# When the reciprocals of the softmax row sums are taken: sixteen quarter-reciprocals per batch, spread over the slots of the attention loop

## The reference, cut to what matters

```python
q, k, v = ...                       # (b, heads 8, t 2048, 32); expert e = tokens e*512..(e+1)*512
attn = jnp.einsum('bhqd,bhkd->bhqk', q, k) * scale
attn = jax.nn.softmax(attn, axis=-1)                      # exp(s - max) / sum
attn_out = jnp.einsum('bhqk,bhkd->bhqd', attn, v)
...
for e in range(4):                  # expert e uses only its first m = 256 >> e columns
    xm = attn_out[:, sl, :m]        # so expert 0 needs 8 heads, 1: 4, 2: 2, 3: 1
    out = jnp.einsum('bnm,om->bno', xm, o_w[:m, :m]) + o_b[:m]
```

## Time and profile before

| | |
|---|---|
| median of three runs | 2130.2 us |
| profiled execution, its own time | 2130.56 us |
| its span, first to last instruction | 2128.7 us |
| mean granted TensorE clock | 0.938 |
| TensorE matmul busy | 1811.4 us, 85% |
| VectorE busy | 1507.0 us, 71% |
| ScalarE busy | 1084.6 us, 51% |
| GpSimd busy | 993.4 us, 47% |

### The profile page before, as it was taken

The page is one execution under the profiler, slowest core; times in us unless marked ns, Lnnn a source line. Parts: engine busy times, 40 slices in busy tenths (PEclk is TensorE's granted clock), DMA queues, the critical chain, the costliest instruction groups (busy, mean ns, idle before and its releaser), DMA issues.

```text
span 2128.7 us, 37884 instructions
## 1 busy us (share of the span) xinstructions
PE 1811.4 (85%) x10752; PEld 1043.2 (49%) x10752; DVE 1507.0 (71%) x2733; ACT 1084.6 (51%) x1998; POOL 993.4 (47%) x654
## 2 busy tenths in 40 slices
PE   4788869999688886999968878699996887789998
PEld 3566434444366543444437654344434664434443
DVE  5688677777478676777648867777755876777774
ACT  0576333666367522566637643256653673326664
POOL 0332345666423245566733313656672332356666
PEclk8899988999899987999979999799997999889999
DMA  3000043010200015201020002500111000350011
GB/s 118 1 0 1 1 158 88 16 43 4 81 1 0 1 38 167 47 11 46 11 71 1 0 1 81 161 12 16 38 51 32 0 0 1 111 134 9 16 39 40
DMA packets 55741, 87.73 MB, mean 41 GB/s; under 512 B 13188, under 2 KB 32004, under 8 KB 52868
## 3 DMA queue, kind: packets, MB, share of 16 engines
q1 hardware_dynamic: 55560, 85.54, 13.8%
HBM read 49.68 MB, written 35.70 MB: 40 GB/s over the span
## 4 chain that ended last, share of the span: by engine, by line
PE 61%; DVE 19%; ACT 8%; issue 7%; DMA 1%; SPq 1%; POOL 1%; DVEq 1%; ACTq 0%; POOLq 0%
PE PS L1119 11%; PE PS L1244 10%; PE PS L1232 9%; PE PS L1257 5%; PE PS L1017 5%; PE PS L1049 4%; DVE MXP L829 4%; DVE XSQ L780 3%; PE PS L1041 3%; ACT XSQ L576 3%; PE PS L1021 3%; PE PS L1162 2%; PE PS L1189 2%; ACT QKT L536 1%; DVE X L732 1%
## 5 line engine op out<-in xcount | busy, mean ns | idle before, releaser
L829 DVE TENSOR_REDUCE MXP<-PS 128x1 f32<-128x512 f32 x960 | 598.9, 681 | 201.9 <-PE PS L1119 198.4
L486 POOL TENSOR_TENSOR TS<-PR 128x1024 f32<-128x1024 f32 (+1 forms) x256 | 573.2, 2239 | 329.3 <-ACT PR L647 329.3
L647 ACT ACTIVATE PR<-PS 128x512 f32<-128x512 f32 x960 | 506.0, 602 | 417.9 <-PE PS L1232 416.4
L1119 PE MATMUL PS<-KOP,QOP 96*128 96x512 f32 x960 | 423.0, 461 | 43.8 <-DMA KOP<-k_scr 30.8
L1232 PE MATMUL PS<-QOP,KOP 97*128 97x512 f32 x960 | 379.8, 409 | 14.5 <-ACT PR L647 9.7
L1119 PEld LDWEIGHTS PS<-KOP,QOP 96*128 96x128 f32 x960 | 191.1, 200 | 298.6 <-DVE MXP L829 224.4
L1244 PE MATMUL PS<-PR,V 128*32 128x512 f32 x1920 | 273.1, 605 | 0.0
L1049 PE MATMUL PS<-PB,QKT 128*128 128x512 f32 x768 | 223.3, 427 | 26.6 <-DVE QKT L760 26.6
L1232 PEld LDWEIGHTS PS<-QOP,KOP 97*128 97x128 f32 x960 | 181.3, 192 | 82.0 <-ACT PR L647 50.6
L443 POOL TENSOR_SCALAR PK<-XSK 128x1024 f32<-128x1024 f32 x64 | 67.1, 1049 | 281.2 <-ACT XSK L562 281.2
L1049 PEld LDWEIGHTS PS<-PB,QKT 128*128 128x128 f32 x768 | 142.2, 192 | 70.0 <-DVE QKT L760 39.4
(11 more groups left out here) (143 smaller groups left out, 2586.6 us busy)
## 6 DMA issues: line engine op xcount, KB each, us to landing
KOP<-k_scr SPq DMA_DIRECT2D x84, 256.0 KB, 6.1
k_scr<-QKS SPq DMA_DIRECT2D x64, 256.0 KB, 2.9
QOP<-q_scr SPq DMA_DIRECT2D x180, 64.0 KB, 2.0
q_scr<-QKS SPq DMA_DIRECT2D x40, 256.0 KB, 3.0
X<-in_L_attn_x_dram SPq DMA_DIRECT2D x16, 512.0 KB, 4.5
out_dram<-X SPq DMA_DIRECT2D x16, 512.0 KB, 3.2
QOP<-MXT SPq DMA_DIRECT2D x240, 0.5 KB
KOP<-k_scr SPq DMA_DIRECT2D x48, 64.0 KB, 2.0
```

The lines of the kernel that those rows point to most:

```text
L486: g.tensor_tensor(sums(k)[:, 0:len(stage)], pair[:, :, 0], pair[:, :, 1], ALU.add).then_inc(S["psum_t"], 1)
L647: a.activation(PR[:, k % 2, w, q], bank(score_bank(p, n, w, q)), ACT.Exp).then_inc(S["ex"], 1)
L829: v.tensor_reduce(MXP[:, u % 2, i, kc:kc + 1], bank(max_bank(p)), AX.X, ALU.max).then_inc(S["am_rd"], 1)
L1119: mm(bank(max_bank(p)), QOP[0:96, u % QS6, i * P:(i + 1) * P], KOP[0:96, h % KS6, kc * CH:(kc + 1) * CH], start=True, stop=True).then_inc( ...
```

## The change

Before, the sixteen quarter-reciprocals of a batch are taken two to a slot: expert 3 in slots 54 and 55, expert 2 in 56 and 57, expert 1 in 58 and 59, expert 0 in 60 and 61. After, one is taken in each of the sixteen slots of PARTS_AT. Each stands behind everything else that the slot has on VectorE but `result`. The slots are 12, 14, 19, 21 for expert 3; 27, 29, 35, 37 for expert 2; 39, 43, 45, 47 for expert 1; 51, 53, 55, 59 for expert 0.

RECIPROCALS now holds the slot of an expert's last quarter. GpSimd's multiplication stands one slot behind it, after that slot's addition: at slots 22, 38, 48 and 60, where it was at 55, 57, 59 and 61. The wait of VectorE for its own `finish` (`c_out`) now asks for the stage that completes the expert; each expert has one such wait, as before. OUT_SLOTS and everything on TensorE and ScalarE is unchanged.

```diff
-    RECIPROCALS = ((3, 54), (2, 56), (1, 58), (0, 60))
+    PARTS_AT = {3: (12, 14, 19, 21), 2: (27, 29, 35, 37), 1: (39, 43, 45, 47), 0: (51, 53, 55, 59)}
+    RECIPROCALS = tuple((z, at[-1]) for z, at in PARTS_AT.items())
+    DONE = {3: 1, 2: 3, 1: 4, 0: 6}
...
-                    for z, at in RECIPROCALS:
-                        if k in (at, at + 1):
-                            if k == at:
-                                dve.wait_ge(S["c_out"], len(stages) * b + len(stages) - 2)
-                            for q in (2 * (k - at), 2 * (k - at) + 1):
-                                divide_part(z, q).then_inc(S["rcp"], 1)
+                    for z, at in PARTS_AT.items():
+                        if k in at:
+                            if k == at[0]:
+                                dve.wait_ge(S["c_out"], len(stages) * b + DONE[z])
+                            divide_part(z, at.index(k)).then_inc(S["rcp"], 1)
```

## The result

The changed kernel takes 2142.0 us (median of five runs, 2140.32 to 2143.79), the kernel before 2131.0 us in the same comparison: a ratio of 1.0053, 95% interval 1.0038 to 1.0067. The forecast was 2138.7 us within 2132.8 to 2144.8, slower. Its profiled execution took 2143.21 us (span 2141.4, mean granted clock 0.936), 12.65 us more than that of before, one execution each. In us the interval of the ratio is 8.1 to 14.3.

What follows compares the result with a forecast made beforehand. The prediction took TensorE to bound the middle slots. Holds behind transposes, 7.9 us, and odd parts, 0.6 us, summed to 8.5 us on 2130.56 us, less 0.36 us to the median: 2138.7 us, range 2132.8 to 2144.8.

Steps and rivals of the forecast that it cites:

- The bound and the wait: In the middle slots TensorE is the bound; M3 waits for M0's read, which may be only 0.14 us late.
- Parts in slots 21, 29, 37, 45: Reciprocals behind a transpose, without slack, delay `values` by 0.47 us, in slot 29 by 0.56: 7.9 us for four batches.
- The insertion: One quarter-reciprocal on VectorE puts the start of the next instruction 0.82 us after its own, ends 0.68 and 0.95 us.
- Odd parts: Reciprocals in slots 19, 27, 35, 39, 43, 47, 51, with 0.58 us free, cost 0.02 us each, 0.6 us in all.
- The rival in which they cost 0.15 us each: Odd parts' reciprocals hold the next reduction for the full 0.95 us: 14.2 us in sum, 2144.4 us; chance 0.16.
- Even parts: Reciprocals in slots 12 and 14 fall before VectorE's 1.44 us of free time and are hidden.
- parts behind slot 53: After reciprocals in slots 53, 55 and 59 no maxima follow, so nothing waits for them.
- GpSimd: Its multiplications at slots 22, 38, 48 and 60 fit into idle gaps, the first three with 0.2 us to spare: cost 0.
- The end of the batch: Removing reciprocals and multiplications from slots 54 to 61 gains 0, with a bound of 0.8 us.
- "Absorbed": Rival: TensorE swallows the stalls, so 16 places cost 0.1 us or so: 1.6 us, 2131.8 us; chance 0.16.
- "faster": Rival: GpSimd's late additions at a batch's end held TensorE or ScalarE; 16 us come back, 2122.7 us; chance 0.06.

Runs made afterwards that it cites:

- experiment 1: Changed kernel with the reciprocals of slots 21, 29, 37, 45 and 53 moved to 20, 28, 36, 44 and 54, none behind a transpose: 2130.95 us.
- experiment 2: Kernel before with only one quarter-reciprocal each moved from the last slots to slots 21, 29, 37 and 45: 2139.39 us, ratio 1.0036.
- experiment 4: Kernel before with two quarter-reciprocals each moved to slots 21, 29, 37 and 45, the other eight left in the last slots: 2153.13 us.
- experiment 7: Changed kernel with negated maximum and transpose deferred behind the four reductions of the next, even slot: 2121.47 us, ratio 0.9942 to the kernel before.
- experiment 3: Changed kernel with all sixteen reciprocals in even slots and GpSimd's multiplications at 18, 34, 44 and 58: 2131.84 us, ratio 1.0007 to the kernel before.
- experiment 5: Kernel before, slot loop untouched, with six added VectorE reductions of 0.7 us ahead of each batch's last result: 2143.64 us, ratio 1.0052.
- experiment 6: Kernel before with negated maximum and transpose deferred behind the four reductions of the next, even slot: 2118.93 us, ratio 0.9937.
- experiment 8: Deferral of experiment 6 on the kernel before, plus finish's second addition moved to a stage's third slot: 2105.34 us, ratio 0.9882.

## Why the prediction was right, and where its sizes were off

*The bound and the wait.* Right. TensorE pays for what holds it in the middle slots, and M3's need of M0's read is where it is held (experiments 1, 2, 4, 7).

*Parts in slots 21, 29, 37, 45.* Forecast 0.47, 0.56, 0.47 and 0.47 us, measured 0.40, 0.55, 0.40 and 0.45, 1.80 for 1.97 us a batch. The insertion held: a reciprocal behind a transpose puts the next read 0.83 us later (0.82 taken). The small excess is in the held slot's tail: `values` starts 1.34 us after the start of M0's read (408.51 to 409.85), where I had taken 1.39 from a slot behind `finish`. The read itself is the difference: directly behind a reciprocal it lasts 0.61 us, in that slot 18 behind a transpose it lasted 0.67. The kernel before, then the changed one:

```profile
391.70 0.67 DVE L829 TENSOR_REDUCE MXP<-PS 128x1 f32<-128x512 f32 x1
```

```profile
408.51 0.61 DVE L831 TENSOR_REDUCE MXP<-PS 128x1 f32<-128x512 f32 x1
```

*Odd parts.* Forecast 0.02 us each, measured none. A reciprocal inserts 0.86 us between two reductions (400.23 to 401.09), more than I took, but the same 1.34 us leave 0.19 us of lateness free, not 0.14. The rival in which they cost 0.15 us each falls: the reciprocal of 0.93 us is followed after 0.86, before its end. The rule behind that rival, that VectorE's next operation waits for the pipe to empty, is how the Trainium skill puts it (page "VectorE: DVE Perf Modes", section "The DRAIN you can't avoid"), and the trace does not agree with it here. The same section of the Trainium skill adds that a next operation which is not held starts earlier, which the prediction left out; the trace agrees with that.

*Even parts, parts behind slot 53, GpSimd.* Right: cost 0 (experiments 1 and 3).

*The end of the batch.* Right that nothing comes back there: slot 57 to behind 63 takes 26.03 us before and after. The stretch that did get shorter, by 1.04 us in three batches and 0.72 in the fourth, is behind it. By the letter this met a sign of being wrong (a stretch from slot 54 on shorter by over 1 us) and missed a sign of being right (unchanged within 0.3 us). But it goes with the clock and not with GpSimd: experiments 1 and 3 have the reciprocals and multiplications moved too, and there the stretch takes 9.41 to 9.74 us in six of eight batches, at clock 0.82, and 8.71 in two, at clock 1.00.

*What the sum lacked.* 8.5 us were forecast, 8.4 measured in the loop, and that they agree so well is partly luck: the foreseen holds make 7.2 us, the odd parts nothing for 0.6, and 0.33 us a batch, 1.3 in all, is the late transpose of slot 37, which I had not foreseen. The measured difference of the medians is 11.0 us, 12.6 in the profiled pair. In the profiled pair the missing term is TensorE's clock: the sum let it be the same before and after, and the profiles show that it moves all the same, as in experiment 5. In the medians this is not shown so firmly: the interval, 8.1 to 14.3 us, holds the loop's 8.4 by itself. What speaks for it there is that all the slower kernels lie above what their changed stretches account for: the changed one by 2.5 us, experiments 2 and 4 by 1.5 and 2.1 us (8.5 for 7.0, 22.2 for 20.1), experiment 5 by about 2, while 1 and 3 stay within 1.3 us of it. "Absorbed" is excluded by experiment 4, and "faster" by the unchanged end.

*Still open.* Why the transpose of slot 37 starts late in the changed kernel and in none of the others. It comes in all four batches, so it belongs to the program's form, but no run varied that. And what shifts the clock's falls from one execution to the next: the first batch differs before any changed instruction has run, and each kernel was profiled in one execution only, so how much of the shift is the kernel's and how much the execution's is not shown.

## What to carry to other kernels

Free time of an engine is free only at the place where it lies: ask of each gap how long it is and who reads the result behind it, before something is put there. VectorE was idle for a quarter of these slots, yet four of sixteen short instructions stood where next to nothing was free, and cost 0.4 to 0.55 us each; one slot earlier they cost nothing. Work in a chain that feeds back to the bounding engine is worth more attention than work at the end: taking two instructions and one addition out of that chain gave 1.2%, where moving the reciprocals to free places gave nothing.

## What the runs showed of the hardware that I had not expected

TensorE's granted clock in one and the same window of unchanged code in the first batch was 1.00 in the kernel before and in experiments 1, 3, 4, 6 and 8, and 0.57 or 0.58 in the changed kernel and in experiments 2, 5 and 7. The stretch behind it took 145.8 to 147.6 us in the former and 148.2 to 148.5 in the latter. Comparing a stretch of two kernels needs the clock of both beside it.

VectorE's reductions take a little less directly behind a reciprocal: four take 2.40 us there and 2.48 us behind idle time, and most of the difference is in the first of them.
